# The second attention of a two-layer kernel: near keys in windows of 96, and part of the far keys made by one-hot products

## The chip, the cores and the metric

One core of one Trainium2 chip runs the whole program. The time is that of one execution on the device in microseconds, the median of three runs. The engines run in parallel, each through its own list of instructions, and wait for each other on semaphores: PE (TensorE, matrix products), DVE (VectorE), ACT (ScalarE), POOL (GpSimd, here only gathers from memory), SP (SyncE, here only plain transfers).

## What is computed

The input is 2048 tokens of 128 numbers. Layer 0 is an attention with 16 heads over all keys and a mixture of experts; layer 1 is an attention with 8 heads over selected keys and a routed network. Only layer 1's attention is touched:

```python
I = sum over 4 index heads of relu(q_i @ k_i) * idx_w      # index score of a query and a key
I = +inf for the 64 nearest keys, -inf for later keys
idx = top_k(I, 96)                                          # 64 near keys, 32 far ones
scores = (q_c . k_c[idx] + q_r . k_r[idx]) * scale          # k_r turned by its rank in idx
out = softmax(scores) @ value[idx] @ W_out
```

(The reference calls `top_k` on each query; queries below 64 take the first 96 keys.)

## The kernel before

The 2048 queries are 16 tiles (`NT`) of 128. A tile is split into 8 groups (`NG`) of 16 queries; a group with its 8 heads is 128 rows, so that one score group is one PSUM bank.

Its near keys come from `near_keys`, by position, and its far keys, 32 per query, from `far`: a buffer of 128 partitions by 32 columns by 64 numbers, a ring of four tiles (`RING`). Column i of it is filled by one indirect gather of POOL (L1622; the first 40 in L1202), which reads 128 rows of `key_table` in memory by a column of `placeT`. Tile 0 has 16 such gathers, each other tile 32: 496. The gathers of a tile wait for its places (`place_ready`) and for the sums of the tile four before (`ctx_full`).

The places come from VectorE: `rank` (L1720 to L1733) takes the best 8, their positions and removes them, four times, over `index`, which PE, ScalarE and VectorE build (`idx`, `relu`, `sum`; L1933, L1675, L1786).

Per tile and group the work is: `q` (PE turns the queries, ScalarE copies them to `qT`), `keys` (VectorE rotates the gathered columns, L1092 to L1098, 16 columns at a time), `far` (PE turns them, ScalarE copies them to `farT`), `score` (PE, L1874 mask, L1876 near keys, L1882 far keys), `max` (VectorE, L1816), `exp` and `norm` (ScalarE), `den` (VectorE), `p` (PE turns the probabilities, ScalarE copies them to `probsT`), `ctx` (PE sums the keys with them, L1894 near and L1899 far, ScalarE copies the sums to `ctxT`), `y` (PE multiplies by the output weights, VectorE adds it to `x`, L1821). `spin` rotates the queries of two tiles.

The order is written out by hand: `selected_schedule(slot, ranking)` gives the work of one slot, a slot being one group, and every engine goes through the list of all slots and does its own share. `index_schedule` spreads ranks and index scores over the first 109 slots of some 138, by an estimated cost. Score banks are three, turn banks two. A group here takes four consecutive queries out of each quarter of the tile, so its near keys span the tile and the one before: `WIN` is 256 columns, and with 128 far columns a score group is 384 wide. SP copies half of `qT` to other partitions once per tile (L1606).

## Time and profile before

| | us |
|---|---|
| median of three runs | 2763.94 (2754.53 to 2770.24) |
| span of the profiled execution | 2263.8 |
| time of the profiled execution beside its span | not recorded |
| first gather starts, last gather starts | 1521.1, 2169.2 |
| first score group of the second attention starts | 1594.6 |
| last result row of the second attention is added | 2216.4 |

The span runs from the first to the last instruction that the profile shows; all positions below are counted from its start. Busy times are sums per engine and overlap each other. "L1622" is a line of the kernel. The clock of PE is granted at one of two levels (1.2 and 2.4 GHz); a window's number is its mean, 1.00 being the higher level.

### The profile page before, as it was taken

How to read it: one execution, taken by the hardware profiler on the slowest of the kernel's cores; microseconds unless marked ns; L12 is line 12 of the kernel's file. 1: busy time of each engine (PE TensorE's matmuls, PEld its weight loads, DVE VectorE, ACT ScalarE, POOL GpSimd, SP SyncE). 2: the span in 40 equal slices, each digit the busy share in tenths (PEclk: the TensorE clock that was granted, in tenths of full speed). 3: DMA queues.
4: the chain of work that ended last, by engine and by line, in shares of the span. 5: the costliest groups of instructions: out<-in, count | busy, mean ns of one | idle time of the engine just before them, and what ended most of it. 6: DMA issues, size and time to landing. Idle time of an engine off the chain costs nothing. (4 is left out here: it accounts for less than half of the span.)

```text
span 2263.8 us, 56900 instructions
## 1 busy us (share of the span) xinstructions
PE 2100.6 (93%) x22674; PEld 1263.2 (56%) x22674; DVE 1789.1 (79%) x3457; ACT 1732.0 (77%) x3507; POOL 1828.5 (81%) x1239
## 2 busy tenths in 40 slices
PE   5899999999999999999999989986999899988878
PEld 1466666666666666666666646652454444444444
DVE  7788888888888888888888658978868986887214
ACT  5798898998989988988989945657566775775543
POOL 4899999999999999999999945627777777777720
PEclk9999999999999999999999989978579996999878
DMA  4000000000000000000000000111211111111101
GB/s 153 1 2 2 2 2 2 2 2 2 2 2 2 2 2 2 2 2 2 2 2 2 2 15 23 39 39 27 52 38 32 38 33 38 31 38 36 39 10 37
DMA packets 44688, 43.19 MB, mean 19 GB/s; under 512 B 21312, under 2 KB 33424, under 8 KB 44176
## 3 DMA queue, kind: packets, MB, share of 16 engines
q1 hardware_dynamic: 28560, 23.35, 3.6%
q0 software_dynamic: 15872, 16.28, 3.1%
q8 instruction: 178, 2.92, 0.5%
q14 instruction: 78, 0.64, 0.1%
HBM read 33.83 MB, written 1.57 MB: 16 GB/s over the span
## 5 line engine op out<-in xcount | busy, mean ns | idle before, releaser
L380 POOL TENSOR_TENSOR probs_lo<-probs,probs_hi 128x1024 f16<-128x1024 f32 x512 | 1076.7, 2129 | 43.0 <-ACT probs L430 42.6
L494 DVE TENSOR_REDUCE part_max<-aux 128x1 f32<-128x512 f32 x1024 | 677.9, 687 | 91.0 <-PE aux L568 86.7
L429 ACT ACTIVATE probs_hi<-scores 128x512 f16<-128x512 f32 x1024 | 630.2, 615 | 134.6 <-PE scores L601 117.3
L430 ACT ACTIVATE probs<-scores 128x512 f32<-128x512 f32 x1024 | 636.6, 622 | 0.0
L1622 POOL DMA_INDIRECT far<-key_table,placeT x456 | 451.9, 991 | 142.9 <-issue 138.7
L617 PE MATMUL acc<-v,probs_hi 128*128 128x65 f16 x4096 | 451.1, 193 | 2.3 <-POOL probs_lo L380 2.3
L619 PE MATMUL acc<-v,probs_hi 128*128 128x64 f16 x4096 | 452.3, 195 | 0.0
L621 PE MATMUL acc<-v,probs_lo 128*128 128x65 f16 x4096 | 450.6, 192 | 0.0
L617 PEld LDWEIGHTS acc<-v,probs_hi 128*128 128x128 f16 x4096 | 382.5, 96 | 82.6 <-POOL probs_lo L380 2.5
L619 PEld LDWEIGHTS acc<-v,probs_hi 128*128 128x128 f16 x4096 | 380.0, 97 | 75.5
L568 PE MATMUL aux<-k_a,q_a 128*128 128x512 f16 x1024 | 392.1, 383 | 5.2 <-DVE roped L480 2.1
L600 PE MATMUL scores<-q_a,k_a 128*128 128x512 f16 x1024 | 388.9, 380 | 6.6 <-ACT probs L430 6.5
L601 PE MATMUL scores<-q_b,k_b 65*128 65x512 f16 x1024 | 390.0, 381 | 0.0
L621 PEld LDWEIGHTS acc<-v,probs_lo 128*128 128x128 f16 x4096 | 381.6, 99 | 0.0
L601 PEld LDWEIGHTS scores<-q_b,k_b 65*128 65x128 f16 x1024 | 100.1, 98 | 112.6 <-issue 0.5
L568 PEld LDWEIGHTS aux<-k_a,q_a 128*128 128x128 f16 x1024 | 100.1, 98 | 83.1 <-DVE part_max L494 13.8
L600 PEld LDWEIGHTS scores<-q_a,k_a 128*128 128x128 f16 x1024 | 100.4, 98 | 81.5 <-ACT probs L430 26.0
L851 POOL TENSOR_TENSOR e_hid_lo<-e_hid,e_hid_hi 128x512 f16<-128x512 f32 x64 | 74.3, 1162 | 61.3 <-ACT e_hid_hi L803 61.3
L472 DVE TENSOR_TENSOR rope_term<-aux,cos 128x512 f32<-128x512 f32 x128 | 88.5, 691 | 26.4 <-PE aux L551 23.4
L1786 DVE SCALAR_TENSOR_TENSOR space<-space,idx_w 128x512 f32<-128x512 f32 (+4 forms) x111 | 72.8, 656 | 44.0 <-ACT space L1675 40.7
L1876 PE MATMUL a_score<-near_keys,qT 64*128 64x256 f32 x256 | 103.6, 489 | 0.0
L480 DVE TENSOR_TENSOR roped<-aux,rope_term 128x512 f32<-128x512 f32 x128 | 88.6, 692 | 17.6 <-DVE aux L475 1.0
(329 smaller groups left out, 3935.5 us busy)
## 6 DMA issues: line engine op xcount, KB each, us to landing
far<-key_table,placeT POOLq DMA_INDIRECT x496, 2.4
qT<-qT SPq DMA_DIRECT2D x16, 256.0 KB, 2.9
e_w<-in_e_w SPq DMA_DIRECT2D x48, 64.0 KB, 1.9
x<-in_x SPq DMA_DIRECT2D x4, 256.0 KB, 3.9
cos<-in_cos SPq DMA_DIRECT2D x1, 1024.0 KB, 6.8
sin<-in_sin SPq DMA_DIRECT2D x1, 1024.0 KB, 8.9
e_w<-in_e_w SPq DMA_DIRECT2D x2, 512.0 KB, 3.9
out<-x SPq DMA_DIRECT2D x4, 256.0 KB, 2.7
```

Source lines behind the costliest of these rows:

```text
L380: pool.tensor_tensor(probs_lo[:, slot], probs[:, wide], probs_hi[:, slot], ALU.subtract).then_inc(low_ready, 1)
L429: act.activation(probs_hi[:, slot, i], bank, ACT.Exp, scale=float(DH0) ** -0.5)
L430: act.activation(probs[:, wide, i], bank, ACT.Exp, scale=float(DH0) ** -0.5).then_inc(probs_ready, 1)
L494: dve.tensor_reduce(part_max[g % 2][:, n % QT, n // QT:n // QT + 1], bank, AX.X, ALU.max).then_inc(aux_free, 1)
L568: ins = pe.matmul(bank, qa[g % QRING][:, t * P:(t + 1) * P], ka[h % 2][:, c * CH:(c + 1) * CH], start=True, stop=True)
L600: pe.matmul(out, ka[h % 2][:, keys], qa[g % QRING][:], start=True, stop=False)
L601: pe.matmul(out, kb[h % 2][:, keys], qb[g % QRING][:], start=False, stop=True).then_inc(scores_ready, 1)
L617: pe.matmul(out, probs_hi[:, n % SLOTS, i, queries], high, start=(kt == 0 and t == 0), stop=False, skip_group_check=True)
L619: pe.matmul(out[:, 0:DH0], probs_hi[:, n % SLOTS, i, queries], low, start=False, stop=False, skip_group_check=True)
L621: ins = pe.matmul(out, probs_lo[:, n % SLOTS, i, queries], high, start=False, stop=(kt == KT0 - 1), skip_group_check=True)
L1622: pool.indirect_dma_start(far[m][:, i, :], None, keep["table"], bass.IndirectOffsetOnAxis(ap=placeT[t % PLACES][:, i:i + 1], axis=0)).then ...
L1876: pe.matmul(b[:, 0:WIN], qT[t % 2][0:KW, 0, 4 * g:4 * g + 4].rearrange("k i a h -> k (i a h)"), near[:, t * P:t * P + WIN], start=False, s ...
```

## The change

A group is now 16 consecutive queries, whose 64 near keys each lie within 96 consecutive ones (`window(t, g)`), so `WIN` is 96 and a score group 224 wide. The near sums use their own copies of these 96 rows (`value`, 96 x 8 x 32, two buffers), which SP loads from `key_table`, 8 transfers per tile. The probabilities are turned in two parts instead of three. The queries of the index are stored in the new order, and the mask and the caps follow it.

For tiles 3 to 9 the last 16 of the 32 far columns, and for tiles 10 to 15 the last 4, are not gathered. SP writes their places (cast to f16 by VectorE) to memory and loads them back, spread over all partitions (`placeB`). VectorE compares them with the key number of each partition (`hot`): one instruction per unit of 4 columns and tile of keys, giving a one-hot matrix in f16 in the index queries' buffer `qi`, a ring of 8 (4 for tile 3). PE multiplies it with the rows split into a high and a low f16 part (`make`), 8 products per key tile, and ScalarE copies the result to `far`. Tiles 3 to 9 have 4 units each, tiles 10 to 15 one; tile t has t + 1 key tiles. So there are 277 comparisons, 2216 products, 34 copies, and 360 gathers instead of 496. `hot` of tile t stands in slots 8t-5 to 8t-2, `make` one slot later.

```diff
 GROUP = 16
 NG = P // GROUP
 HALF = NG // 2
-WIN = 2 * P
+WIN = KTS
 SC = WIN + P
...
+def window(t, g):
+    return max(t * P + GROUP * (g + 1) - WIN, 0)
...
+PER = 4
+UNITS = {t: 4 if t < 10 else 1 for t in range(3, NT)}
+MADE = sorted(UNITS)
+MADE_AT = 3 - NG
+SPLIT = MADE[-1] + 1
+SPLIT_AFTER = ("exp", 1, 0)
...
-    sums = {2: [("p", c, 0)], 3: [("p", c, 2), ("p", c, 4)], 4: [("ctx", c, 0)], 6: [("p", c, 1), ("p", c, 3)],
-            7: [("p", c, 5), ("ctx", c, 1)]}
+    sums = {2: [("p", c, 0)], 3: [("p", c, 2)], 4: [("ctx", c, 0)], 6: [("p", c, 1)], 7: [("p", c, 3), ("ctx", c, 1)]}
...
+    made = j - 1 - MADE_AT
+    work += [("make", made // NG, made % NG)] if made % NG < UNITS.get(made // NG, 0) else []
...
+    t = (j - MADE_AT) // NG
+    work += [("hot", t, (j - MADE_AT) % NG)] if (j - MADE_AT) % NG < UNITS.get(t, 0) else []
...
+def made(t):
+    return PER * UNITS.get(t, 0)
 def gather_list():
-    return [(t, i) for t in range(NT) for i in range(gathers(t))]
+    return [(t, i) for t in range(NT) for i in range(gathers(t) - made(t))]
...
 def landed(t, half):
-    return 256 * (t // RING + (0 if t % RING == 0 and half else 1))
+    each = lambda s: 16 if not half else 16 - made(s) if s else 0
+    return 16 * sum(each(s) for s in range(t % RING, t + 1, RING))
...
+        spare = QN[:, 0:3].rearrange("p t h c -> p (t h c)").bitcast(F16)
+        split = spare[:, 0:SPLIT * 2 * KW].rearrange("p (t k) -> p t k", t=SPLIT)
+        placeB = spare[:, SPLIT * 2 * KW:SPLIT * 2 * KW + P * max(made(t) for t in MADE)]
         biggest = sb("biggest", [P, NG], F32)
         den = sb("a1_den", [P, NG], F32)
...
+                def spread_places(t):
+                    n, b = MADE.index(t), P // 32
+                    out = dram["places"][n:n + 1, 0:made(t) * P]
+                    sp.wait_ge(place16_ready, n + 1)
+                    for k in range(b):
+                        sp.dma_start(out[0].rearrange("(i b r) -> b i r", i=made(t), b=b)[k],
+                                     place16[n % PLACES][32 * (k + 1) - made(t):32 * (k + 1), :]).then_inc(place_out, 16)
+                    sp.wait_ge(place_out, (n + 1) * b * 16)
+                    if n == 0:
+                        sp.wait_ge(turn_free, free_no["q", 2, 3])
+                    else:
+                        sp.wait_ge(hot_ready, hot_no[t, 0, 0] - 1)
+                    sp.dma_start(placeB[:, 0:made(t) * P], out.broadcast_to([P, made(t) * P])).then_inc(placeB_in, 16)
...
+                    if t >= 2:
+                        sp.wait_ge(ctx_full, 2 * (t - 1))
+                    for g in range(NG):
+                        sp.dma_start(value[t % 2][:, g, :], keep["table"][window(t, g):window(t, g) + WIN, 0:CKV]
+                                     ).then_inc(value_in, 16)
+                    if t + 1 in UNITS:
+                        spread_places(t + 1)
...
-                        ins = act.activation(qT[t % 2][0:KW, 1 - i // 2, :, :, half].rearrange("k i a h -> k h a i"),
-                                             src[0:KW, :].rearrange("k (h a i) -> k h a i", h=4, a=4), ACT.Copy)
+                        ins = act.activation(qT[t % 2][0:KW, 1 - i // 2, :, :, half].rearrange("k i a h -> k h (i a)"),
+                                             src[0:KW, :].rearrange("k (h q) -> k h q", h=4), ACT.Copy)
...
+                    elif kind == "make":
+                        if i == 0:
+                            if t >= RING:
+                                act.wait_ge(ctx_full, 2 * (t - RING + 1))
+                        first = FAR - made(t) + PER * i
+                        ins = act.activation(far[t % RING][:, first:first + PER, :],
+                                             src[:, 0:PER * KW].rearrange("p (i k) -> p i k", i=PER), ACT.Copy)
...
+                        act.activation(split[:, :, 0:KW], rows[:, 0:SPLIT, :], ACT.Copy).then_inc(high_ready, 1)
...
-                        half = ctxT.rearrange("c h (a i) -> c i a h", a=4)[:, 16 * i:16 * i + 16]
-                        sums = ctxp.rearrange("c (i a h) -> c i a h", a=4, h=H1)
-                        for a in range(4):
-                            ins = act.activation(half[:, :, a], sums[:, :, a], ACT.Copy)
-                        ins.then_inc(ctx_copied, 1)
+                        half = slice(i * P // 2, (i + 1) * P // 2)
+                        act.activation(ctxT[:, :, half], ctxp.rearrange("c (q h) -> c h q", h=H1), ACT.Copy
+                                       ).then_inc(ctx_copied, 1)
...
+                            dve.tensor_copy(place16[n % PLACES][:], place[:]).then_inc(place16_ready, 1)
...
+                def hot(t, k):
+                    if k == 0:
+                        dve.wait_ge(placeB_in, 16 * (MADE.index(t) + 1))
+                        dve.wait_ge(idx_full, idx_no["idx", ring_of(t) - 1, len(index_chunks(ring_of(t) - 1)) * NIDX - 1])
+                    for kt in range(t + 1):
+                        o = hot_no[t, k, kt] - hot_no[t, 0, 0]
+                        if o >= ring_of(t):
+                            wait_used(dve, *hots[hot_no[t, k, kt] - 1 - ring_of(t)])
+                        elif o == 0 and t > MADE[0]:
+                            wait_used(dve, *hots[hot_no[t, 0, 0] - 2])
+                        dve.tensor_scalar(hot_tile(t, k, kt), placeB[:, k * CH:(k + 1) * CH], key_id[:, kt:kt + 1], None,
+                                          ALU.is_equal).then_inc(hot_ready, 1)
...
+                        if i and t in UNITS:
+                            dve.wait_ge(turn_free, free_no["make", t, UNITS[t] - 1])
...
+                def make_keys(b, t, k):
+                    if k == 0:
+                        pe.wait_ge(split_ready, 1)
+                    for kt in range(t + 1):
+                        pe.wait_ge(hot_ready, hot_no[t, k, kt])
+                        for part in range(2):
+                            for i in range(PER):
+                                ins = pe.matmul(b[:, i * KW:(i + 1) * KW], hot_tile(t, k, kt)[:, i * P:(i + 1) * P],
+                                                split[:, kt, part * KW:(part + 1) * KW], start=(kt + part + i == 0),
+                                                stop=(kt == t and part == 1), skip_group_check=True)
+                        if kt < t:
+                            ins.then_inc(hot_used, 1)
+                    return ins
...
-                    pe.matmul(b[:, 0:SC], keep["unit"][:].bitcast(BF16), mask[:, g, :].bitcast(BF16), start=True,
-                              stop=False, skip_group_check=True)
+                    pe.matmul(b[:, 0:SC], keep["unit"][:].bitcast(BF16), mask[:, NG if t else g, :].bitcast(BF16),
+                              start=True, stop=False, skip_group_check=True)
                     pe.matmul(b[:, 0:WIN], qT[t % 2][0:KW, 0, 4 * g:4 * g + 4].rearrange("k i a h -> k (i a h)"),
-                              near[:, t * P:t * P + WIN], start=False, stop=False, skip_group_check=True)
+                              near[:, window(t, g):window(t, g) + WIN], start=False, stop=False, skip_group_check=True)
...
-                    parts = [1] if t == 0 else [0, 1]
-                    for part in parts:
-                        pe.matmul(out, rows[:, t - 1 + part, 0:CKV],
-                                  probsT[:, part, HALF * c:HALF * c + HALF, :].rearrange("p g l -> p (g l)"),
-                                  start=(part == parts[0]), stop=False, skip_group_check=True)
+                    for j in range(HALF):
+                        g = HALF * c + j
+                        pe.matmul(ctxp[:, j * P:(j + 1) * P], value[t % 2][:, g, :], probsT[0:WIN, 0, g, :],
+                                  start=(j == 0), stop=False, skip_group_check=True)
```

## Rows read from the trace of the kernel before

**Rows 1.** Head and busy line of the page: busy us (share) xinstructions
```profile
span 2263.8 us, 56900 instructions
PE 2100.6 (93%) x22674; PEld 1263.2 (56%) x22674; DVE 1789.1 (79%) x3457; ACT 1732.0 (77%) x3507; POOL 1828.5 (81%) x1239
```

**Rows 2.** Groups of the page: out<-in xcount | busy us, mean ns | idle before
```profile
L1622 POOL DMA_INDIRECT far<-key_table,placeT x456 | 451.9, 991 | 142.9 <-issue 138.7
```

**Rows 3.** Waits of VectorE, from 1594 to 2076 us, then to 2217 us: us, times, longest
```profile
DVE space L1786 <- ACT space L1675: 40.3, 31, 3.2
DVE x L1821 <- PE a_turn L1858: 34.3, 7, 9.8
...
DVE far_turned L1092 <- DMA far<-key_table,placeT: 56.5, 5, 13.3
```

**Rows 4.** Windows: length, busy us of PE, PEld, DVE, ACT, POOL; clock, DMA, GB/s
```profile
1594.00:1673.00 79.00, 74.89 (x398) 36.28 (x399) 59.55 (x130) 45.18 (x101) 60.72 (x61) 0.63 0.18 44
1673.00:1941.00 268.00, 246.09 (x1790) 131.58 (x1788) 218.83 (x399) 185.78 (x427) 204.92 (x208) 0.88 0.16 35
1941.00:2076.00 135.00, 121.83 (x990) 66.87 (x989) 117.93 (x191) 97.00 (x223) 103.37 (x104) 0.97 0.15 35
2076.00:2217.00 141.00, 108.17 (x796) 61.38 (x797) 39.42 (x129) 69.23 (x165) 71.81 (x74) 0.79 0.11 25
1749.00:1784.00 35.00, 31.61 (x257) 17.21 (x256) 32.55 (x61) 26.65 (x62) 26.78 (x28) 1.00 0.17 39
1856.00:1902.00 46.00, 41.61 (x258) 21.55 (x258) 32.09 (x56) 27.92 (x66) 35.33 (x36) 0.73 0.14 32
2009.00:2042.00 33.00, 30.06 (x248) 16.52 (x249) 27.94 (x47) 24.81 (x58) 25.25 (x25) 1.00 0.16 35
```

**Rows 5.** Timeline of PE at full clock: near sums, one score group, a turn
```profile
1808.35 1.90 PE L1894 MATMUL a_ctx<-a_probsT,rows 128*32 128x512 f32 x4 [1.80 <-ACT a_probsT L1645]
1810.09 1.18 PE L1899 MATMUL a_ctx<-a_probsT,far 128*32 128x32 f32 x32
...
1812.42 0.34 PE L1874 MATMUL a_score<-mask,unit 128*128 128x384 bf16 x1
1812.69 0.70 PE L1876 MATMUL a_score<-near_keys,qT 64*128 64x256 f32 x2
1813.31 0.42 PE L1882 MATMUL a_score<-farT,qT 64*32 64x128 f32 x8
...
1782.99 0.66 PE L1852 MATMUL a_turn<-ident,far 128*128 128x128 f32 x4
```

**Rows 6.** Timeline of PE in the first attention: first of 24 f16 products, and what follows
```profile
699.95 0.19 PE L617 MATMUL acc<-v,probs_hi 128*128 128x65 f16 x1
...
700.69 0.38 PE L568 MATMUL aux<-k_a,q_a 128*128 128x512 f16 x1
```

**Rows 7.** Groups of VectorE by shape: busy us, mean ns | idle before
```profile
L1816 DVE TENSOR_REDUCE biggest<-a_score 128x1 f32<-128x384 f32 x128 | 69.6, 545 | 8.0 <-PE a_score L1882 7.9
L1786 DVE SCALAR_TENSOR_TENSOR space<-space,idx_w 128x512 f32<-128x512 f32 x72 | 53.4, 742 | 29.6 <-ACT space L1675 28.1 <-DVE space L1786 0.5
L98 DVE TENSOR_SCALAR e_xn<-x,mv,rstd 128x128 f32<-128x128 f32 x16 | 4.2, 341 | 0.0
L1278 DVE COPY far<-rows 128x512 f32<-128x512 f32 x1 | 0.4, 422 | 0.0
L951 DVE TENSOR_SCALAR gate_s<-gate_s 128x256 f32<-128x256 f32 x1 | 0.3, 295 | 0.0
```

**Rows 8.** Waits of SyncE's queue, 1594 to 2217 us
```profile
SPq L1606 <- ACT qT L1636: 497.7, 15, 47.8
```

**Rows 9.** The tile far: ns min/median/max, first and last start us
```profile
L1622 POOL DMA_INDIRECT far<-key_table,placeT x456: 938/944/1962, 1579.6 to 2169.2; - x152
L1098 DVE TENSOR_TENSOR far<-far_turned,far_swapped x31: 691/692/693, 1580.4 to 2172.9; 128x512 f32<-128x512 f32 x31
```

**Rows 10.** The tile placeT: the same columns
```profile
L1733 DVE STREAM_TRANSPOSE placeT<-place x13: 192/211/213, 1598.1 to 2083.2; 128x32 uint32<-128x32 uint32 x13
```

More of the change, by code:

```diff
@@ L1128, in projections1 @@
         first_bank = [ps(f"first_bank{i}", [P, CH], F32) for i in range(2)]
-        first_full, first_relued, first_scaled, first_summed, flip = (sem("first_" + n) for n in (
-            "full", "relued", "scaled", "summed", "flip"))
+        first_full, first_relued, first_scaled, first_summed = (sem("first_" + n) for n in (
+            "full", "relued", "scaled", "summed"))
         far, placeT, place_ready, far_in, angle, angles_in, queries_ready, rows_ready, table_out = (
@@ L1317, in first_rank @@
                             own.link(dve.match_replace(values, first_top[:], values, -3.4e38))
-                    if t:
-                        dve.transpose(placeT[t][:], first_place[:]).then_inc(place_ready, 1)
-                        return
-                    dve.transpose(flipped[:], first_place[:]).then_inc(flip, 1)
-                    dve.wait_ge(flip, 1)
-                    for b in range(4):
-                        part = slice(P // 2 + 32 * (b // 2), P // 2 + 32 * (b // 2) + 32)
-                        ins = dve.tensor_copy(placeT[0][32 * b:32 * b + 32, 0:16],
-                                              flipped[part, 16 * (b % 2):16 * (b % 2) + 16])
-                        if b < 3:
-                            own.mark(ins)
-                        else:
-                            own.wait()
-                            ins.then_inc(place_ready, 1)
+                    dve.transpose(placeT[t][:], first_place[:]).then_inc(place_ready, 1)
                 for n, (kind, i) in enumerate(jobs):
@@ L1555, in selected_attention @@
             keep[n] for n in ("rows", "queries", "near_keys", "nout", "ctxT", "qi", "ki_hi", "ki_lo", "mask"))
+        value = [sb(f"near_value{i}", [WIN, NG, CKV], F32) for i in range(2)]
         space, ahead = keep["space"], keep["ahead"]
@@ L1590, in selected_attention, with ring_of, hot_tile, wait_used @@
         rotations = [w for w in schedule if w[0] in ("keys", "spin")]
+        hots = [(t, k, kt) for t in MADE for k in range(UNITS[t]) for kt in range(t + 1)]
+        hot_no = {h: n + 1 for n, h in enumerate(hots)}
+        inner_no = {h: n + 1 for n, h in enumerate(h for h in hots if h[2] < h[0])}
+        def ring_of(t):
+            return NIDX * (2 if t > MADE[0] else 1)
+        def hot_tile(t, k, kt):
+            e = (k * (t + 1) + kt) % ring_of(t)
+            return qi[:, e % NIDX, (e // NIDX) * CH:(e // NIDX + 1) * CH]
+        def wait_used(eng, t, k, kt):
+            if kt < t:
+                eng.wait_ge(hot_used, inner_no[t, k, kt])
+            else:
+                eng.wait_ge(turn_full, turn_no["make", t, k])
         with nc.Block() as block:
@@ L1854, in fill_turn @@
                             g = HALF * (i % 2) + j
-                            ins = pe.transpose(out, probs[:, g, (i // 2) * P:(i // 2 + 1) * P], ident[:])
+                            keys = slice(WIN, SC) if i // 2 else slice(0, WIN)
+                            ins = pe.transpose(out[0:keys.stop - keys.start, :], probs[:, g, keys], ident[:])
                     if kind == "y":
@@ L2202, in tables @@
     t["cap0"] = np.where(k <= l - LW, 3.4e38, np.where(k <= l, -3.3e38, -1e36 * (k + 1))).astype(f32)
-    row = np.arange(P)
-    i4, quarter = row // 32, row % 32 // H1
-    l = (32 * quarter + i4)[:, None, None] + 4 * np.arange(NG)[None, :, None]
-    s = np.arange(WIN)[None, None, :] - P
-    gathered = np.broadcast_to(np.arange(P)[None, None, :] // FAR == quarter[:, None, None], (P, NG, P))
-    first_gathered = (l >= LW) & (np.arange(P)[None, None, :] // FAR == (l - LW) // 16)
-    first = np.where(l < LW, (s >= 0) & (s < KTS), (s > l - LW) & (s <= l))
-    rest = (s > l - LW) & (s <= l)
-    for name, keep in (("mask_first", [first, first_gathered]), ("mask", [rest, gathered])):
-        t[name] = bfloat16(np.where(np.concatenate(keep, 2), 0.0, -1e30))
+    block = (row % 32 // H1)[:, None, None]
+    l = (4 * (row // 32))[:, None, None] + block + GROUP * np.arange(NG + 1)[None, :, None]
+    s = np.array([window(0, g) for g in range(NG)] + [P + GROUP - WIN])[None, :, None] + np.arange(WIN)[None, None, :]
+    first = (l < LW) & (np.arange(NG + 1) < NG)[None, :, None]
+    near = np.where(first, (s >= 0) & (s < KTS), (s > l - LW) & (s <= l))
+    far = (np.arange(P)[None, None, :] // FAR == block) & ~first
+    t["mask"] = bfloat16(np.where(np.concatenate([near, far], 2), 0.0, -1e30))
     t["unit"] = bfloat16(np.eye(P))
+    t["key_id"] = (P * np.arange(SPLIT)[None, :] + np.arange(P)[:, None]).astype(f32)
     t["iota"] = np.tile(np.arange(E0, dtype=f32), (P, 1))
@@ L2282 @@
     dram["out"] = nc.dram_tensor("out_0", (T, D), F32, kind="ExternalOutput").ap()
+    dram["places"] = nc.dram_tensor("places", (len(MADE), P * max(made(t) for t in MADE)), F16, kind="Internal").ap()
     dram["key_table"] = nc.dram_tensor("key_table", (T, KW), F32, kind="Internal").ap()
```

79 lines of the change are left out of this document (52 added, 27 removed).

## The prediction

> **What bounds the kernel now.** I read the page first, then the waits, then one row per tile of the second attention. The page says PE is busy 93% and POOL 81% [rows 1], and POOL gathers until 2169 us [rows 9]; the 456 gathers of the main loop take 991 ns each, and of the 142.9 us before them 138.7 us is issue, not a wait [rows 2]. So a gather costs (451.9 + 142.9) / 456 = 1.30 us, the 32 of a tile 41.7 us, and it is tempting to call POOL the bound. The waits of VectorE say otherwise. From 1594 us (first score group) to 2076 us it waits for PE and ScalarE alone; only from 2076 us does it wait for a gather, 5 times, 56.5 us [rows 3]. A tile needs less than 41.7 us, POOL started three tiles earlier, and tiles 13 to 15 catch up with it. Until then the work is held by PE and VectorE: with the clock granted full, a tile took 35 us where VectorE had 32.55 us of work, and 33 us where it had 27.94 and PE 30.06; with a clock of 0.73 one took 46 us [rows 4]. ScalarE is at 69% (185.78 of 268 us).
>
> I cut the attention into four stretches (tiles 0-1, 2-8, 9-12, 13-15 with the drain): 79, 268, 135 and 141 us, with VectorE busy 59.55, 218.83, 117.93 and 39.42 us [rows 4]. The first runs at 0.63 of the clock with PE busy 95%: it is PE's. The next two are both engines'. The last waits for gathers.
>
> **PE, per tile at full clock.** Removed: near scores go from 256 to 96 columns. The pair took 1813.31 - 1812.69 = 0.62 us [rows 5]; its column rate I take from the near sums, four records of 512 columns in 1810.09 - 1808.35 = 1.74 us, 0.85 ns a column and record [rows 5]. 160 columns less in two records are 0.27 us. The mask product loses 160 columns of one record, at most 0.07 us. Eight groups: 2.7 us. Near sums: two halves of 1.74 us become two of half as many columns, -1.7 us, and four short products for one long one cost some of it back (-1.5 us taken). Two of six turns of probs go, four transposes each: the turn of far keys, of the same form, is busy 0.66 us [rows 5], of which the next instruction overlaps some; 0.50 us each, -1.0 us. Together -5.2 us of some 31.
>
> Added: the one-hot products. There are (t+1) key tiles per unit, four units for t = 3 to 9 (4 x 49 = 196) and one for t = 10 to 15 (81): 277 steps of 8 f16 products with a 128x128 weight and 64 columns. 24 such pairs took 700.69 - 699.95 = 0.74 us [rows 6], so 31 ns each, 0.25 us a step, 69 us in all: 7 us per tile for t = 3 to 9, 3.4 us after. PE ends a little above its old load in the second stretch, and 2 us under it in the third.
>
> **VectorE.** The row maximum reads 224 instead of 384 columns of PSUM: 545 ns [rows 7] less 160 columns at 1.04 ns (the 742 ns of 512 columns against a fixed part of some 0.2 us [rows 7]) is about 378 ns, 1.3 us a tile. The cast of the places adds 0.2 us. The big term is the 277 comparisons `is_equal`, 128x512 f16 to f16 with one scalar per partition; the trace has none. Bounds by the nearest rows: as many elements in f32 take 422 ns as a copy and 256 take 295 ns [rows 7], two elements a ns, whatever the fixed part. 512 f16 elements are the bytes of 256 f32: 295 ns. Two pointer scalars cost 341 - 231 = 110 ns over the same line at 128 columns, one 55 ns [rows 7]; and those 16 instructions took 4.2 us, 262 ns each, so a row of independent ones overlaps by 80 ns [rows 7]. By bytes: 295 + 55 - 80 = 0.27 us. By elements: 422 + 55 - 80 = 0.40 us. At the rate of one element, as the 742 ns row: 0.67 us. I take 0.27, for it is a copy-like instruction with SBUF on both sides, and keep 0.27 to 0.67.
>
> The Trainium skill ("VectorE: DVE Perf Modes", the perf-mode tier table) lets tensor_scalar on 16-bit SBUF data run at four elements a cycle, fp32 at two. The two f32 rows above agree with the fp32 half of it; no row shows the other. By that page the sum would be the one by bytes.
>
> **ScalarE** loses 160 columns in exp and in the normalisation, two copies of probs and six of eight context copies a tile, and gains one to four copies of 256 columns. It falls from 69%; its waits are VectorE's largest before 2076 us (40.3 us [rows 3]), so they should shrink.
>
> **Queues.** POOL: 112 + 24 = 136 gathers fewer, -177 us; it will wait for its ring (ctx_full), which nobody feels: tile 15's gathers may start after tile 11's sums, some 16 slots of 4.4 us before they are used, and take 28 x 1.3 = 36 us. SP: per tile 8 value loads, then 4 stores of places, a wait for them, a wait for the last comparison of the tile before, a broadcast load; all stand ahead of the next qT copy. SP now sits idle 497.7 of 623 us, waiting for qT [rows 8]. From the value load (slot 8t-2) to the first comparison (8t+3) there are 5 slots, 22 us, for three round trips of a DMA, which I estimate at 13 us together. The rank that the places come from lies ahead: the last is done at 2083 us [rows 10], in slot 109 at the latest, and its comparisons stand in slot 115. Cost nothing; if the cover went, each tile would be late by what the chain takes beyond 22 us. The split of rows (one copy, one subtraction) is 2 us, once.
>
> **The sum.** Stretch 1: PE's loss of 5.2 us at 0.63 clock, two tiles, shared with VectorE: -8 us. Stretch 2: VectorE 218.8 - 9.1 + 1.4 + 196 x 0.27 = 264.0 us, 37.7 a tile; with the 2.5 us of idle that its fullest tile shows [rows 4], 7 x 40.2 = 281: +13 us. The comparisons stand in four of eight slots, beside key rotations and spins, and three score banks carry only two or three slots; from t = 8 on there are more key tiles than the ring of 8, so VectorE also waits for PE in mid-unit: +8 us. Stretch 3: 117.9 - 5.2 + 50 x 0.27 = 126.2, plus 4 x 2.5: 136, +1 us. Stretch 4: VectorE has nothing, the 56.5 us of gather waits go, PE's 22 us a tile leave 27 with stalls: 3 x 27 + 20 for the drain = 101 against 141, -40 us. Sum -26 us. The profiled execution has a span of 2263.8 us [rows 1]; its own time outside the span is not recorded, and the median of the three runs is 2763.94 us, 500.1 us more. I leave that part as it is: 2238 us of span, 2738 us.
>
> **Rivals.**
> A. The comparison runs by elements, 0.40 us: 0.13 x 246 comparisons in stretches 2 and 3 = +32 us, 2770 us. For it: the f32 rows show nothing above two elements per ns. Against: bytes.
> B. It runs at one element, 0.67 us: 0.40 x 246 = +98 us, 2836 us. This is the case on the other side: VectorE's comparisons become the bound, and it decides from 26 / 246 = 0.11 us above my price, that is from 0.38 us each. For it: most rows of VectorE with 512 columns are 0.69 to 0.75 us. Against: the f32 TENSOR_SCALAR with 256 columns at 295 ns.
> C. PE and ScalarE are so much lighter that VectorE's waits of stretch 2 and 3 vanish: stretch 2 ends at 264 us (-4), stretch 3 at PE's 4 x 32 us (-7), stretch 4 loses ten more, so -8 - 4 - 7 - 50 = -69 us, 2695 us. For it: 74.6 us of those waits are for PE and ScalarE [rows 3]. Against: the work of a tile is lumpy.
> D. PE, now waiting for comparisons, falls to the half clock more often. A tile at 0.73 costs 46 against 35 us [rows 4]; three more such tiles, +33 us: 2771 us.
> E. VectorE and POOL exclude each other. The rotation's add, with two SBUF inputs, has 691/692/693 ns in 31 cases, in a stretch where POOL is never without a gather for more than 0.3 us, while gathers reach 1962 ns over a median of 944 [rows 9]: the gather yields, not VectorE. If VectorE yielded for comparisons, half a gather in the 40% of the time in which one runs, 0.19 x 277 = +50 us: 2788 us. The Trainium skill ("SBUF — State Buffer", the shared port pair) says that a two-port VectorE instruction and GpSimd lock each other out for the whole instruction, whoever came first; by it E would be so where a gather came first. The trace shows the stretched gather, and nothing of the other direction.
>
> That the change does not do what it says (the made columns wait for something else and gathers still bind): 136 gathers fewer end 177 us before 2170 us, so I give it nothing of its own.
>
> **Chances.** Forecast 42%, C 18%, A 10%, B 14%, D 11%, E 5%. Range: 2685 to 2805 us leaves out B and the end of C. The forecast's own range is 2715 to 2758. With 0.5% (13.8 us, about what a measurement can tell) as the bound: faster, under 2750: 37 + 18 + 4 = 59%; same: 19%; slower: 22%.
>
> **What would show it.** Comparison rows near 350 ns with 0.27 us from start to start; no VectorE wait for a gather; POOL with idle time that waits for PE's sums; stretch 2 at about 289 us and the end from tile 13 on at 101 us. Wrong if comparisons take 0.5 us or more, if the stretch of tiles 2 to 8 does not grow, or if SP's chain makes VectorE wait for placeB.

## The result, and the profile after

| | us |
|---|---|
| before, median of 4 | 2767.09 (2754.53 to 2772.1) |
| after, median of 4 | 2656.94 (2646.33 to 2666.9) |
| ratio | 0.9592, 95% interval 0.9552 to 0.9633 |
| forecast | 2738, range 2685 to 2805 |

The change is faster, as was likelier, but by 110 us and not by 26, and the time lies below the range. The profiled execution of the changed kernel has a span of 2657.1 us and took 2658.91 us: 1.8 us lie outside the span, not 500.

The page of the changed kernel: head, busy line, then PE and its clock in 40 slices.

```profile
span 2657.1 us, 61608 instructions
PE 2161.2 (81%) x24894; PEld 1376.9 (52%) x24894; DVE 1846.0 (69%) x3743; ACT 1685.7 (63%) x3414; POOL 1685.1 (63%) x1103
...
PE   6899999999999999999899843677666755554488
...
PEclk8999999999999999999989775566677766676688
```

Against [rows 1] the engines have about the same work, but the span is 393 us longer than the one that the prediction was read from, and PE's busy digits fall from 9 to between 3 and 7 in slices 24 to 38, the end of the projections and the second attention. The waits of the changed kernel (us, times, longest), of all engines from 1594 to 2600 us and of VectorE to 2611 us:

```profile
POOL far L1681 <- PE a_ctx L2011: 454.4, 11, 66.5
ACT far L1706 <- PE a_turn L1932: 131.0, 28, 39.7
PEld a_turn L1932 <- issue: 113.7, 93, 4.8
ACT farT L1700 <- remote: 102.0, 5, 44.6
...
DVE a_den L1920 <- ACT a_probs L1757: 112.3, 22, 27.3
DVE biggest L1912 <- remote: 82.4, 7, 27.2
DVE space L1880 <- ACT space L1745: 78.2, 35, 13.4
DVE qi L1853 <- PE a_turn L1932: 22.7, 6, 6.5
```

Answering [rows 3], the wait for gathers is gone. In its place POOL, ScalarE and VectorE wait up to 27 to 66 us at a time. POOL's wait for the sums of the ring is the one that the prediction expected; part of the others is for "remote", a releaser that the trace doesn't name. The groups that answer to [rows 2, 7] (busy us, mean ns | idle before):

```profile
L1853 DVE TENSOR_SCALAR qi<-queries,key_id 128x512 f16<-128x512 f16 x277 | 76.4, 347 | 69.7 <-remote 47.1 <-PE a_turn L1932 22.7
L1912 DVE TENSOR_REDUCE biggest<-a_score 128x1 f32<-128x224 f32 x128 | 48.8, 382 | 93.8 <-remote 82.4 <-PE a_score L1994 11.2
L1681 POOL DMA_INDIRECT far<-key_table,placeT x320 | 309.8, 968 | 623.3 <-PE a_ctx L2011 454.4 <-issue 94.7 <-DVE placeT L1806 45.8
```

And two pieces of its timeline: a row of comparisons, then PE's score group, which answers to [rows 5].

```profile
2039.77 1.40 DVE L1853 TENSOR_SCALAR qi<-queries,key_id 128x512 f16<-128x512 f16 x5
...
2099.55 0.27 PE L1986 MATMUL a_score<-mask,unit 128*128 128x224 bf16 x1
2099.75 0.46 PE L1988 MATMUL a_score<-near_keys,qT 64*128 64x96 f32 x2
2100.14 0.42 PE L1994 MATMUL a_score<-farT,qT 64*32 64x128 f32 x8
```

These two prices were right: a comparison is 347 ns, and five in 1.40 us are (1.40 - 0.35) / 4 = 0.26 us each (0.27 forecast); the row maximum takes 382 ns (378). What was wrong lay elsewhere.

### The profile page after: what moved, and what is told of

It is laid out like the page before. It is cut to its first block and busy times, and to the rows that moved or that the text cites. A ratio compares the mean times of both kernels' runs of the same rounds, so it can differ in the third digit from the quotient of the medians.

```text
span 2657.1 us, 61608 instructions
## 1 busy us (share of the span) xinstructions
PE 2161.2 (81%) x24894; PEld 1376.9 (52%) x24894; DVE 1846.0 (69%) x3743; ACT 1685.7 (63%) x3414; POOL 1685.1 (63%) x1103
## 5 line engine op out<-in xcount | busy, mean ns | idle before, releaser
L1681 POOL DMA_INDIRECT far<-key_table,placeT x320 | 309.8, 968 | 623.3 <-PE a_ctx L2011 454.4
L1932 PE MATMUL a_turn<-queries,qi 128*128 128x64 f16 x2216 | 98.0, 205 | 105.3 <-issue 85.8
L1706 ACT ACTIVATE far<-a_turn 128x256 f32<-128x256 f32 x34 | 13.0, 383 | 250.9 <-PE a_turn L1932 131.0
L1986 PE MATMUL a_score<-mask,unit 128*128 128x224 bf16 x128 | 39.0, 305 | 141.6 <-ACT a_probs L1757 78.8
L1932 PEld LDWEIGHTS a_turn<-queries,qi 128*128 128x128 f16 x2216 | 86.1, 105 | 118.4 <-issue 113.7
L1700 ACT ACTIVATE farT<-a_turn 128x512 f32<-128x512 f32 x64 | 38.1, 596 | 170.5 <-remote 102.0
```

The lines of the kernel that those rows point to most:

```text
L1681: pool.indirect_dma_start(far[m][:, i, :], None, keep["table"], bass.IndirectOffsetOnAxis(ap=place_of(placeT, t, i), axis=0)).then_inc(far ...
L1932: ins = pe.matmul(b[:, i * KW:(i + 1) * KW], hot_tile(t, k, kt)[:, i * P:(i + 1) * P], split[:, kt, part * KW:(part + 1) * KW], start=(kt ...
```

## The experiments

The runs were timed in batches, each on one chip within some minutes. The unchanged kernel stands in every batch, and it turned out to have two levels, one for a whole batch:

| batch | before, us | runs timed in it |
|---|---|---|
| result | 2767.1 | the changed kernel |
| 1 | 2757.2 | e1, e2, e3 |
| 2 | 2774.0 | e4 to e7 |
| 3 | 2265.0 | e8 to e11 |
| 4 | 2756.8 | e12 to e14 |
| 5 | 2759.9 | e15, e16 |
| 6 | 2264.1 | e17 |
| 7 | 2265.5 | e18 |

I call 2757 to 2774 us the held level and 2264 to 2266 us the free level. The expectations from e12 on speak of chips of a first and a second kind; that was too much said, since batches 3 and 4 ran on a chip of the same number. What sets the level stays open.

**e1, nothing changed, profiled again.**

> The kernel before, unchanged, once more with its profile. The profile that the prediction was read from has a span of 2263.8 us, 500 us under the times of the same kernel, while the profile of the changed kernel has 2657.1 us, 2 us under its time, and in it ScalarE stands still for 19 to 40 us whenever POOL issues a row of gathers. Theory S: the executions that were timed of the kernel before hold the same stalls, the profile that I read did not; expected span about 2762 us, the second attention about 1140 us long instead of 640, and engines idle while POOL gathers. Rival T: the 500 us lie outside the span (before the first or behind the last instruction); expected span about 2264 us again and a time of 2764 us.

2753.85 us (2749.61 to 2759.13), span 2752.2 in an execution of 2753.74 us. So theory S holds. The first profile, 2263.8 us, is of an execution at the free level, 500 us shorter than those that were timed; up to the first gather (1521.1 and 1521.7 us) the two traces agree. Waits of all engines in e1, 1594 to 2700 us:

```profile
POOL far L1622 <- PE a_ctx L1899: 377.8, 11, 70.1
DVE biggest L1816 <- remote: 251.9, 23, 28.1
ACT a_probsT L1645 <- remote: 182.0, 13, 27.1
ACT farT L1641 <- remote: 179.8, 13, 64.2
POOL far L1622 <- issue: 135.1, 443, 0.3
```

The windows of e1 (columns as [rows 4]) show when: within a row of gathers, between two rows, in the first 7 us of a row, and in its rest.

```profile
1642.00:1692.00 50.00, 0.00 (x0) 0.00 (x0) 2.43 (x6) 0.00 (x0) 37.80 (x41) 0.50 0.13 26
1714.00:1762.00 48.00, 44.17 (x274) 21.13 (x272) 41.37 (x89) 32.42 (x73) 0.00 (x0) 0.72 0.08 23
1763.00:1770.00 7.00, 6.76 (x53) 4.31 (x53) 2.75 (x7) 3.23 (x8) 5.48 (x6) 1.00 0.11 23
1770.00:1803.00 33.00, 7.79 (x35) 3.32 (x33) 7.75 (x16) 4.20 (x10) 24.81 (x27) 0.53 0.13 26
```

PE and ScalarE do nothing for 50 us while POOL gathers; without gathers PE is busy 92%. This row starts harmlessly, and the others stop some 7 us into it. The timeline of e1 at that point:

```profile
1768.45 0.42 PE L1882 MATMUL a_score<-farT,qT 64*32 64x128 f32 x8
...
1768.80 0.66 PE L1852 MATMUL a_turn<-ident,far 128*128 128x128 f32 x4
...
1770.02 0.54 ACT L1675 ACTIVATE space<-a_idx 128x448 f32<-128x448 f32 x1
...
1779.88 0.56 DVE L1816 TENSOR_REDUCE biggest<-a_score 128x1 f32<-128x384 f32 x1 [4.12 <-remote]
...
1784.77 0.60 ACT L1641 ACTIVATE farT<-a_turn 128x512 f32<-128x512 f32 x1 [14.21 <-remote]
```

The scores' products start at 1768.45, and the maximum that waits for them at 1779.88; the turn starts at 1768.80, and ScalarE, idle from 1770.56, empties it at 1784.77. What comes late is what TensorE hands over. I paired the k-th score group with the k-th maximum and took the waits above 0.3 us. The 23 for "remote" ended 4 to 65 us after the scores as modelled, all of which fall inside a row of gathers; the 13 others that ended with the scores' own signal did so within 0.07 us, all outside rows. Where VectorE waited for ScalarE's sum (L1824) inside a row, it started 0.03 us after it, 10 times of 10. Whether the products themselves or their signals are late the trace can't say, since the ends of matmuls are modelled. So a tile costs a row of gathers (41 us in which little else runs) and then some 30 us of work, 65 to 77 us in all for tiles 1 to 12, where the free level's trace has 33 to 42.

**e2, regrouping alone** (`UNITS = {15: 1}`: 492 gathers, 16 comparisons) and **e3, 16 made columns in tiles 3 to 15** (`UNITS = {t: 4 for t in range(3, NT)}`: 288 gathers, 520 comparisons).

> The changed kernel with only one unit of one-hot products left, that of tile 15 (UNITS = {15: 1}): 492 gathers instead of 360, 16 comparisons instead of 277; groups, near keys and value loads as changed. Theory S (gathers hold the other engines back, some 0.8 us each over their own cost): 132 gathers more than the changed kernel cost up to 132 x 0.8 = 105 us, so 2740 to 2765 us: the regrouping alone gains under 25 us. Rival R (the narrower groups made the gain, the one-hot products are neutral): 2640 to 2680 us.

> The changed kernel with four units for tiles 10 to 15 too: 288 gathers instead of 360, 520 comparisons instead of 277. Theory S: 72 gathers fewer give 58 us back, 243 comparisons at 0.27 us cost 66 us of VectorE where it is not held up by gathers, so 2600 to 2670 us. Rival V (VectorE is the bound, as the prediction had it): 2657 + 66 = 2723 us or more.

e2: 2695.34 us, ratio 0.9785 (0.9701 to 0.9869), 62 us less (by the interval 36 to 82), with only 4 gathers fewer; between both expectations and in neither. e3: 2630.57 us, ratio 0.955 (0.9458 to 0.9641), as theory S had it: 243 comparisons more and 72 gathers fewer than the changed kernel, and no slower. Under the held level a gather is worth more than the comparisons that replace it.

**e4, the same transfers without row numbers; e5, the same bytes from SP's queue.** In e4 from tile 4 on:

```
-pool.indirect_dma_start(far[m][:, i, :], None, keep["table"], IndirectOffsetOnAxis(...))
+pool.dma_start(far[m][:, i, :], keep["table"][i % NT * P:i % NT * P + P, :])
```

> The kernel before, but from tile 4 on each of the 32 gathers of a tile is a plain copy of 128 consecutive table rows into the same column, issued by the same engine (GpSimd) at the same place with the same waits: same bytes, same count, no list of row numbers. The far columns of tiles 4 to 15 therefore hold other keys than the reference asks for. Theory I (it is the indirect form that holds up the other engines while a row of gathers is issued): second attention falls by about 45 us for each of 12 tiles less what POOL still takes, 2250 to 2400 us. Theory Q (any transfer whose descriptors GpSimd makes does it): 2650 to 2760 us, as the unchanged kernel's 2753.8. A shorter issue than the gathers' 0.95 us would show as shorter rows: then Q scales with the row's length.

> The kernel before, but from tile 4 on the 32 far columns of a tile are filled by two transfers of 16 columns each that SP issues from consecutive table rows (same bytes to the same places, two tiles ahead); GpSimd issues nothing there. The far columns of tiles 4 to 15 hold other keys than the reference asks for. Theories I and Q (what GpSimd issues is what holds up the rest): 2230 to 2330 us, since the compute alone ran a tile in about 42 us in the first profile. Theory B (the bytes that land in SBUF beside the compute hold it up, from whatever queue): above 2600 us.

e4: 2344.39 us, ratio 0.8455 (0.8424 to 0.8485); e5: 2347.25 us, ratio 0.8465 (0.8439 to 0.8491). The group of e4's plain copies:

```profile
L1627 POOL DMA_DIRECT2D far<-key_table x384 | 203.0, 543 | 303.1 <-PE a_ctx L1903 268.2 <-DVE placeT L1737 31.2 <-issue 3.6
```

As many transfers of as many bytes, issued by the same engine closer together, hold nothing up: it is the indirect form. Theories Q and B fall. The windows of e4 for tiles 1 to 7, 8 to 11 and 12 to 15, cut at the additions of result rows (columns as [rows 4]):

```profile
1766.60:2034.50 267.90, 242.16 (x1785) 128.64 (x1784) 218.51 (x398) 183.79 (x420) 117.86 (x224) 0.90 0.14 37
2034.50:2174.10 139.60, 125.26 (x1009) 68.74 (x1008) 121.62 (x199) 100.96 (x229) 64.35 (x122) 0.97 0.14 39
2174.10:2298.10 124.00, 106.50 (x804) 61.98 (x804) 41.70 (x134) 69.40 (x165) 16.90 (x32) 0.79 0.07 17
```

The free level's trace has 267.2, 139.5 and 142.1 us there. So in a batch at the held level, tiles 1 to 11 take the free level's time to within 1 us once their gathers are gone. The 82 us that e5 keeps above 2265 lie ahead of them: tile 0 is done at 1766.9 us in e4, at 1667.9 at the free level, and the 112 gathers that are left stand there. The last stretch is 18 us shorter than at the free level, for nothing waits for a gather.

Taking away 384 gathers gave 2774.0 - 2347.3 = 426.7 us, 1.11 us a gather, or 1.06 without those 18 us; one takes 1.25 us in a row. The 500.1 us that the prediction could not place are 1.01 us for each of the 496 gathers.

**e6, e7: the gathers in small portions** (with 16 made columns in tiles 3 to 15, and on the kernel before):

```
+each = -(-(gathers(t) - made(t)) // NG)
+if t >= RING and i % each == 0:
+    pool.wait_ge(score_full, NG * (t - RING + 1) + 4 + i // each)
```

> The version with 16 made columns in each of the tiles 3 to 15 (16 gathers a tile, 2630.6 us), but GpSimd issues them two at a time, each pair after another score group, and not in a row of 20 us. Theory L (a hold-up builds up only after some 8 us of gathers issued back to back, since in the traces the first 8 us of a row ran at full speed): the stops vanish, 2250 to 2400 us. Theory E (every gather holds the others up for its own 1.25 us, wherever it stands): 2600 to 2660 us, as the row.

> The kernel before, with its 32 gathers a tile issued four at a time (5 us), each four after another score group, from tile 4 on. Theory L: four gathers end before the 8 us that a hold-up needs, but a group of the compute is hardly longer than 5 us, so the gathers nearly touch: 2350 to 2600 us. Theory E: 2740 to 2800 us, as the unchanged kernel or slightly worse, since a pause is now put between the fours.

e6: 2530.2 us, ratio 0.9125 (0.9098 to 0.9151), 100 us under e3 but not 2250 to 2400. e7: 2681.17 us, ratio 0.9669 (0.9641 to 0.9697), 81 us above theory L's range and 59 under theory E's. The trace of e6 says why: after each wait for the ring the score groups waited for are past, and 8 gathers still go in one row, in whose 14 us ScalarE works 1.25 us:

```profile
2142.20:2156.20 14.00, 8.45 (x115) 6.54 (x114) 5.35 (x15) 1.25 (x2) 7.61 (x8) 0.75 0.20 42
```

**e8, e9, e13, e14, e15: portions that start three groups later** (`+ 7` for `+ 4`, from tile 2 on). e8 and e13 are one kernel, with 16 made columns; e9 has its gathers singly; e14 regroups alone; e15 is the kernel before with these lines and nothing else.

> The version with 16 made columns in tiles 3 to 15 and its gathers in pairs, each pair behind a later score group than in the run at 2530.2 us (whose traces still show rows of 8 gathers, 9.8 us, after each wait for the ring, with 12.6 to 13.8 us of idle ScalarE): the pairs now start after the wait has cleared, and tiles 2 and 3 are spaced too. Theory L (a hold-up builds up within a row): without rows of 8 some 10 us a tile come back, 2370 to 2450 us. Theory E (each gather costs its own time wherever it stands): 2500 to 2540 us.

> The same, and of each pair the second gather waits for a later event of the same group (a normalised row of weights), so that gathers of tiles 3 to 15 come one at a time where the work allows. Theory L: at or a little under the run in pairs, 0 to 40 us. Theory E: the same time as the run in pairs, within 10 us. If pairs already leave nothing to hold, both give the same.

> 16 made columns in tiles 3 to 15, gathers in pairs behind later score groups, tiles 2 and 3 spaced too. On a chip of the first kind theory L (a hold-up builds up within a row, and the rows of 8 are gone): 2380 to 2470 us, against 2530 us with rows of 8 left; theory E (each gather costs its own time): 2510 to 2550 us. On a chip of the second kind: 2335 to 2350 us, as before (2340.9).

> Regrouping alone (made columns only in tile 15), its 32 gathers a tile spaced four to a score group. On a chip of the first kind: 2600 to 2660 us by theory L and E alike, since fours at 5 us each nearly touch (2681 us for the kernel before with the same spacing, less the 60 us of the regrouping). On a chip of the second kind: theory R (regrouping takes work off the engines that set the pace and the spacing costs nothing there) 2190 to 2230 us, the best time of all; theory W (the spacing starves the ring of far columns) above 2250 us.

> The kernel before with nothing changed but a wait ahead of each four gathers (tiles 2 to 15), on a score group three later than in the run at 2681 us, so that no row of 8 or more follows the wait for the ring. On a chip of the first kind: theory L 2480 to 2560 us (the regrouped version with the same spacing took 2463, and regrouping was worth 60 to 75 us); theory E above 2650 us. On a chip of the second kind: 2262 to 2285 us, as unchanged.

At the held level, e13 took 2418.92 us (ratio 0.8787, 0.8763 to 0.8812), e14 2462.66 (0.893, 0.8907 to 0.8952) and e15 2489.52 (0.9019, 0.8991 to 0.9046). Theory E's times fall for all three, theory L's hold for e13 and e15, and e14 is 137 us under what both gave. For e15 only the number holds: the portions still touch, and 344 of the 456 gathers of its main loop go in rows of 8 to 24, less than 0.6 us apart (e1: all 456; e7: 420). In e13 it is 48 of 240, and there the mechanism shows. These are the windows of e8 and e13, one kernel at the free and at the held level, for tiles 1 to 11:

```profile
1661.00:2162.70 501.70, 424.87 (x5944) 314.27 (x5942) 435.68 (x1002) 255.70 (x603) 175.49 (x176) 0.89 0.15 34
1698.00:2213.60 515.60, 430.54 (x5946) 316.60 (x5944) 435.03 (x1003) 255.01 (x603) 180.13 (x175) 0.88 0.14 33
```

With pairs some 176 gathers cost 14 us more at the held level, 0.08 us each instead of 1. Of the 74 us between the two spans 37 lie ahead, up to the end of tile 0, where the first 40 gathers still go in one row, and 23 in tiles 12 to 15, for which I have no reason.

Why fours that nearly touch do so well was not tried. The waits of e15 (1594 to 2441 us) suggest that the portions wait for TensorE's own scores, so that gathers which hold TensorE's signals up hold themselves up, and stop:

```profile
DVE x L1824 <- PE a_turn L1861: 136.1, 16, 19.8
POOL far L1625 <- issue: 121.8, 394, 1.0
POOL far L1625 <- PE a_score L1885: 112.6, 36, 8.4
```

One wait ahead of each portion is worth 270 us, twice the 134 us that the change gave in the same batch, without a gather fewer. e8 fell into a free batch, 2340.9 us (ratio 1.0334, 1.0311 to 1.0357), and e9 with it, 2345.29 (1.0353, 1.0318 to 1.0389): single gathers gave nothing there, and at the held level they were not tried.

**e10 and e11: the changed kernel and regrouping alone, with e4's plain copies**, against the kernel before.

> The changed kernel, with every gather of tiles 4 to 15 replaced by a plain copy of 128 consecutive table rows into the same column (same count, place and waits; those columns hold other keys than the reference asks for). It stands against the kernel before with the same edit, 2344.4 us. Theory P (the blind sum, -26 us, was right for a chip on which gathers hold nothing up, and the rest of the measured -110 us is fewer stops): 2290 to 2330 us. Theory G (the change gains its 4% whether or not gathers hold anything up): 2235 to 2262 us.

> Regrouping alone (made columns only in tile 15), with every gather of tiles 4 to 15 replaced by a plain copy of consecutive rows, against 2344.4 us of the kernel before with the same edit. Its measured gain with real gathers was 72 to 62 us. Theory P: most of that gain is shorter exposure to the stops, and 15 to 45 us remain, 2300 to 2330 us; made columns then cost 0 to 20 us on top of it, where they gained 40 with real gathers. Theory G: 60 us or more remain, 2285 us or less.

Both fell into a free batch, so they stand against 2265.0 us with real gathers, not against e4, and the theories, written for the held level, can't be judged. e10: 2282.12 us, ratio 1.0076 (1.005 to 1.0102). e11: 2206.91 us, 0.9722 (0.9666 to 0.9779). Regrouping and plain copies together gain 58 us. By e4 the plain copies alone take 18 us off the last stretch, which leaves some 40 us to regrouping, an estimate. Making the columns costs 75.2 us (e10 less e11, both with plain copies). At the free level the changed kernel is slower than the one before by 17 us, where the sum had -26.

**e12, e16, the changed kernel again; e17, the same with spaced gathers; e18, e14 again.**

> The changed kernel, unchanged, beside the kernel before on the same chip. On a chip where the kernel before takes 2750 to 2775 us: 2645 to 2670 us again (ratio 0.959). On a chip where it takes 2262 to 2269 us: theory P (the blind sum holds where nothing is held up) 2225 to 2255 us, ratio 0.985 to 0.995; theory C (the made columns and the 8 value loads a tile cost more than the sum gave, as the run with plain copies, 2282 us, hints): 2275 to 2300 us, ratio 1.005 to 1.015.

> The changed kernel beside the unchanged one. On a chip of the first kind: ratio 0.955 to 0.960, as twice before. On a chip of the second kind: theory P (blind sum) ratio 0.985 to 0.995; theory C (made columns and value loads cost more than the sum gave) 1.005 to 1.015.

> The changed kernel with the spacing of the run at 2489.5 us: 16 gathers in pairs in tiles 4 to 9, 28 in fours in tiles 10 to 15. It lies between the spaced regrouping alone (2462.7) and the spaced version with 16 made columns everywhere (2418.9). Theory L: 2425 to 2460 us. Theory P (the blind sum of -26 us for the change holds once the rows are broken): 2489.5 - 26 = 2463, so 2450 to 2475 us. Above 2480 us neither. On a chip of the second kind: 2270 to 2300 us.

> Regrouping alone (made columns only in tile 15), its 32 gathers a tile spaced four to a score group. On a chip of the second kind (unchanged 2262 to 2269 us): theory R (the gathers run beside the rest there, so real ones cost what plain copies did, 2206.9 us, and the made columns are what costs the change its gain) 2195 to 2225 us; theory W (the spacing starves the ring of far columns where nothing is held up) 2240 us or more. On a chip of the first kind: 2455 to 2470 us again.

e12: 2631.58 us, ratio 0.9555 (0.9514 to 0.9596), and e16: 2625.66, 0.9518 (0.9484 to 0.9553), both held: a little under what I expected. e17 fell into a free batch: 2284.2 us, ratio 1.0073 (1.0048 to 1.0098), with real gathers what e10 was with copies. e18, free: 2264.09 us, ratio 0.9989 (0.9979 to 1.0), theory W's number but not its reason. A wait of VectorE and one of POOL (1594 to 2220 us):

```profile
DVE far_turned L1097 <- DMA far<-key_table,placeT: 115.9, 19, 14.2
POOL far L1684 <- PE a_score L1997: 9.6, 8, 7.4
```

The portions hold POOL up by 9.6 us in all, and still VectorE waits 115.9 us for gathers. Its tiles 6 to 13 take 40.9 to 43.8 us each, 32 gathers of 1.3 us. So regrouped and spaced, the free level is POOL's, and the 57 us between e11 and e18 are mostly the gathers' own pace. Regrouping with real gathers and without the spacing never ran at the free level. The three kernels that ran at both levels:

| | gathers | free | held |
|---|---|---|---|
| before | 496 | 2265.0 | 2757 to 2774 |
| regrouped, spaced (e18, e14) | 492 | 2264.1 | 2462.7 |
| 16 made columns, spaced (e8, e13) | 288 | 2340.9 | 2418.9 |

Of the versions that ran at both levels the regrouped, spaced one is the only one that beats or equals the kernel before at both, and at the held level it beats the changed kernel, 2462.7 us against 2625.7 to 2656.9. The kernel before with spacing alone (e15, 2489.5 held) did not run at the free level. With 16 made columns 44 us more are to be had at the held level, for 77 us lost at the free one.

## Why the prediction was wrong

**The step that failed: "its own time outside the span is not recorded ... I leave that part as it is".** I took 500.1 us between the span and the median for something outside the attention that the change doesn't touch. It lay inside: the trace was of the free level, the timed runs of the held one, and the 500 us are what 496 gathers hold up. (The spans of the three timed runs are not recorded; in every execution recorded later, the kernel before at 2749 us and more among them, time and span lie within 2.9 us.) The levels of the kernel before are 492 to 509 us apart, 0.99 to 1.03 us a gather, and the change takes 136 gathers away: 135 to 140 us. With the 17 to 20 us that it costs at the free level (e10, e17) this makes -115 to -122 us, against -110, -125 and -134 measured. The count of gathers is not the whole account, since regrouping with 4 gathers fewer already took 62 of these us. No rival held any of this. The rows spoke of it only as the mismatch itself: 2263.8 us [rows 1] against 2754.53 at the least.

**The sum within the span was wrong too, by 43 to 46 us.** At the free level I compare e17 and e10 with the first trace, from one addition of a result row to another (L1821 and its like: tiles 0, 7, 11 and 15; 1667.6, 1934.8, 2074.3 and 2216.4 us before, each within 7 us of the prediction's cuts). e17 has spaced gathers and e10 plain copies; the changed kernel itself never ran at the free level.

| stretch, tiles | before | forecast | e17 | e10 |
|---|---|---|---|---|
| to tile 0 | 73.6 | -8 | -9.1 | -8.0 |
| 1 to 7 | 267.2 | +21 | +42.8 | +37.2 |
| 8 to 11 | 139.5 | +1 | +10.6 | +5.6 |
| 12 to 15 | 142.1 | -40 | -17.7 | -20.6 |

The windows of e17 at these cuts (columns as [rows 4]) and, under them, those of e11 for tiles 1 to 7 and 12 to 15:

```profile
1658.50:1968.50 310.00, 269.16 (x3348) 193.89 (x3347) 265.05 (x603) 166.03 (x391) 126.32 (x127) 0.84 0.16 36
1968.50:2118.60 150.10, 133.71 (x1413) 90.61 (x1413) 131.19 (x251) 87.39 (x203) 112.31 (x108) 0.84 0.21 40
2118.60:2243.00 124.40, 108.31 (x1060) 81.86 (x1052) 45.94 (x165) 55.96 (x137) 27.97 (x29) 0.64 0.10 21
```

```profile
1663.00:1908.00 245.00, 225.24 (x1781) 142.29 (x1781) 208.85 (x398) 157.12 (x364) 131.94 (x243) 0.78 0.18 46
2048.00:2167.00 119.00, 101.11 (x932) 76.33 (x932) 42.68 (x151) 55.15 (x134) 14.73 (x28) 0.66 0.08 20
```

- *The comparisons' price, 0.27 us, and VectorE's sum.* Right: 264.0 us forecast for tiles 1 to 7, 265.05 measured. Rivals A and B are out. The bytes decided, and the rule of the Trainium skill ("VectorE: DVE Perf Modes", the perf-mode tier table) that I put beside the sum agrees with these 0.26 us.
- *The idle time beside it: "2.5 us ... 7 x 40.2", and +8.* Too small: 16 to 22 us of the 43 to 46. I took one tile's 2.5 us, from the fullest tile, for all, where the seven tiles together had 268 - 218.83 = 49 us of idle VectorE [rows 4]. Regrouping alone left 245 - 208.85 = 36 us of idle VectorE in tiles 1 to 7; the comparisons added 53 us of work and 59 us of time (304 in e10), so idle came to 42 to 45 us, where I had 25.5. That the comparisons come in lumps behind which TensorE's next group waits would explain it, but was not tried.
- *Stretch 4: "the 56.5 us of gather waits go", "3 x 27 + 20".* The same size of miss, 19 to 22 us. The waits went, as said, but they were worth less: e4, the old groups with nothing left to wait for, took 124.0 us there instead of 142.1. The 22 us beyond these 18 were to come from a lighter PE and did not come: three tiles of e17 took 33.4, 37.2 and 33.5 us and the drain 20.4. PE is busy 108.31 of 124.4 us at a mean clock of 0.64, where e4 has 106.50 at 0.79; my 27 us had PE at full clock. Rival D had a lower clock, but from waiting for comparisons, and e11, with comparisons in tile 15 alone, has 0.66 in this stretch. What lowers it was not tried.
- *Queues.* Right at both levels: SP's extra work stays under its wait for qT (513.8 us in the changed kernel, 497.7 in [rows 8], 193.9 left in e17), and VectorE waits for no placeB. The 13 us for the chain had no row behind them; in e17 the first such chain issues its last load 7 us after its first (1653.7 and 1660.6 us), and the comparisons start at 1678.0.
- *Rival E.* The mean comparison lasts 345 ns beside plain copies (e10), 347 in the changed kernel and 359 in e17, with real gathers at the free level: 14 ns of the 190 that it had. Comparisons held up by a gather are there, though: the 128 comparisons of e17 that overlap a gather take 375 ns on the mean and up to 552, the 149 others 345 and at most 353.
- *"It gives nothing of its own"* for 136 gathers fewer: at the free level that is not contradicted; at the held level the change would gain nothing without it, for its arithmetic costs 75 us (at the free level) and regrouping gave 62.

That the sign came out right was luck: where the sum was meant to hold, the change is slower, and the gain comes from a step outside the sum. Of what was said would show it wrong, "if the stretch of tiles 2 to 8 does not grow" was met at the held level: tiles 1 to 7 take 457 us in the changed kernel and 505 in e1. That tells of the level, not of the prices.

## What to carry to other kernels

Before reading a trace for prices, hold its span against the execution times: 500 us apart means that it shows another machine than the one that is timed, and the difference is no constant that can be carried over. Where indirect gathers stand in long rows (in e1 the others stopped some 7 us into one) beside work in which TensorE hands over often, look for engines that idle for "remote" inside the rows, and try to break the rows with a wait on that work's own progress before replacing gathers by arithmetic: here the wait gave 270 us, the arithmetic (e14 to e13) 44. Price a lump of new work on an engine together with the idle time that its stretch already has, taken over the whole stretch and not from its fullest tile.

## What the runs showed of the hardware that was not expected

- The same program on the same kind of chip has two levels, 2264 to 2266 and 2757 to 2774 us, steady within a batch of some minutes (13 runs within 2261 to 2269, 9 within 2753 to 2763). They differ only where indirect gathers run: 1521 us up to the first one at both, and tiles 1 to 11 in 407 us with plain copies at the held level as with gathers at the free one. The same chip number appeared with both; nothing that was run says what switches them.
- At the held level an indirect gather (128 rows, issued each 1.25 us) in rows of 32 costs the program 1.0 to 1.1 us, and in pairs (e13) 0.08 us in tiles 1 to 11; a plain copy of the same size from the same engine, 0.54 us busy, costs nothing that can be measured beside SP's transfers (2344.4 and 2347.3 us).
- In e1 the hold-up falls on what TensorE releases (23 maxima 4 to 65 us late); ScalarE's signals to VectorE pass in 0.03 us in the same rows. The cause behind it stays open: a delay of the products or of their signals.
- Beside a gather a comparison of VectorE lasts up to 552 ns, without one at most 353 (e17).
- The same kernel gave ratios of 0.9592, 0.9555 and 0.9518 in three held batches, the third's interval only just touching the first's: the size of a hold-up may differ a little between batches too.
